# A product with V taken in five visits of a step instead of six, in an attention and mixture-of-experts layer

## The reference, cut to what matters

```python
x = _layernorm(resid_stream, ln_w, ln_b)                  # 4 x 1024 tokens, 128 wide
q = jnp.einsum('bsd,hde->bshe', x, W_q) + b_q             # 16 heads of 64
k = jnp.einsum('bsd,hde->bshe', x, W_k) + b_k
v = jnp.einsum('bsd,hde->bshe', x, W_v) + b_v
scores = jnp.einsum('bqhe,bkhe->bhqk', q, k) * scale
scores = jnp.where(causal, scores, -jnp.inf)              # a query sees keys up to its own
pattern = jax.nn.softmax(scores, axis=-1)
z = jnp.einsum('bhqk,bkhe->bqhe', pattern, v)
attn_out = jnp.einsum('bqhe,hed->bqd', z, W_o) + b_o
```

## Time and profile before

| What | Value |
|---|---|
| median of 3 runs | 1194.63 us (1191.52 to 1194.76) |
| the profiled execution's own time | 1196.98 us |
| its span, first to last instruction | 1195.3 us |
| mean granted TensorE clock | 0.971 of 2.4 GHz |
| busy share of the span | PE 91%, DVE 77%, ACT 59%, POOL 53% |
| chain that ended last, by engine | PE 73%, DVE 10%, DMA 6% |

### The profile page before, as it was taken

One profiled execution on the slowest core, in us unless ns is written; L12 is line 12 of the kernel. 1 busy time (PEld: TensorE's weight loads), 2 busy tenths in 40 slices (PEclk: granted clock), 3 DMA queues, 4 the chain that ended last, 5 costly groups with the idle time before them and its releaser, 6 DMA issues.

```text
span 1195.3 us, 51556 instructions
## 1 busy us (share of the span) xinstructions
PE 1085.8 (91%) x19964; PEld 776.9 (65%) x19964; DVE 916.5 (77%) x2215; ACT 710.1 (59%) x1489; POOL 629.1 (53%) x634
## 2 busy tenths in 40 slices
PE   4799999999999999999999999999999557999995
PEld 2567777777777777677777777777776445445442
DVE  7878888888888888788888888888888573565653
ACT  4656666656666666566656665666666243576663
POOL 5866666565656665656555555555566121023232
PEclk8899999999999999999999999999999877999997
DMA  8667776666777767677777776677777530000000
GB/s 186 169 169 168 179 169 163 163 163 163 169 174 167 171 163 172 161 172 171 173 172 171 165 169 163 163 163 174 168 171 170 125 68 10 1 10 18 9 10 25
DMA packets 121358, 164.53 MB, mean 138 GB/s; under 512 B 44272, under 2 KB 55536, under 8 KB 121328
## 3 DMA queue, kind: packets, MB, share of 16 engines
q1 hardware_dynamic: 121328, 164.15, 58.1%
HBM read 109.28 MB, written 21.23 MB: 109 GB/s over the span
## 4 chain that ended last, share of the span: by engine, by line
PE 73%; DVE 10%; DMA 6%; issue 5%; ACT 3%; SPq 2%; POOL 1%; DVEq 0%; ACTq 0%; POOLq 0%
PE ZB L622 25%; PE SPS L605 13%; PE SPS L606 10%; DMA XTB<-xt_scratch 5%; DVE PTZ L914 5%; PE ZB L590 5%; PE ZB L595 5%; PE ZB L800 3%; PE ZB L630 2%; PE SPS L792 2%; DVE SSB L974 2%; SPq L415 1%; PE ZB L784 1%; PE ZB L818 1%; PE SPS L757 1%
## 5 line engine op out<-in xcount | busy, mean ns | idle before, releaser
L974 DVE CUSTOM_DVE_ANT_0 SSB<-SPS,MASK 128x640 f32<-128x640 f32 (+7 forms) x512 | 374.1, 747 | 149.5 <-PE SPS L606 126.5
L605 PE MATMUL SPS<-KHP,QS 128*128 (+2 forms) x768 | 330.0, 434 | 33.5 <-DVE NM L974 28.1
L1283 ACT ACTIVATE PRL<-SSB,NM 128x640 f32<-128x640 f32 (+3 forms) x256 | 252.7, 987 | 161.2 <-DVE NM L974 98.2
L622 PE MATMUL ZB<-PTZ,VR 32*64 32x256 f32 (+2 forms) x16384 | 329.5, 296 | 18.9 <-DVE PTZ L914 18.9
L622 PEld LDWEIGHTS ZB<-PTZ,VR 32*64 32x64 f32 x16384 | 265.2, 131 | 73.3 <-issue 58.7
L459 POOL TENSOR_TENSOR X<-X,OT 128x512 f32 (+1 forms) x64 | 82.0, 1281 | 355.2 <-ACT OT L1293 346.7
L606 PE MATMUL SPS<-KLP,QS 128*128 (+2 forms) x768 | 261.4, 349 | 0.0
L914 DVE STREAM_TRANSPOSE PTZ<-PRL 128x640 f32<-128x640 f32 (+3 forms) x256 | 255.1, 1025 | 0.0
L605 PEld LDWEIGHTS SPS<-KHP,QS 128*128 128x128 f32 x768 | 145.7, 190 | 123.2 <-issue 58.5
L1283 ACT ACTIVATE PRS<-SSB,NM 128x128 f32<-128x128 f32 (+3 forms) x256 | 142.2, 556 | 118.1 <-DVE NM L974 117.7
L442 POOL TENSOR_TENSOR QS<-RAW,QS 64x512 fp32r<-64x512 f32 x128 | 165.1, 1290 | 10.3
(11 more groups left out here) (171 smaller groups left out, 1085.6 us busy)
## 6 DMA issues: line engine op xcount, KB each, us to landing
VR<-v_scratch SPq DMA_DIRECT2D x256, 256.0 KB, 5.5
KHP<-KHP SPq DMA_DIRECT2D x64, 256.0 KB, 3.2
KLP<-KLP SPq DMA_DIRECT2D x64, 256.0 KB, 3.9
v_scratch<-V SPq DMA_DIRECT2D x32, 512.0 KB, 7.6
RSB<-rcp_scratch SPq DMA_DIRECT2D x64, 256.0 KB, 3.9
XTB<-xt_scratch SPq DMA_DIRECT2D x62, 256.0 KB, 3.2
WQK<-in_W_q SPq DMA_DIRECT2D x33, 64.0 KB
WQK<-in_W_k SPq DMA_DIRECT2D x33, 64.0 KB
```

The source lines that it names most:

```text
L605: pe.matmul(SP_[n % 2][:, c0:c0 + wc], q, kh[:, c0:c0 + wc], start=True, stop=False)
L622: last = pe.matmul(ZB[h * DH:(h + 1) * DH, i, kt * TR:QT * TR], VR[rows, j, kt, h * DH:(h + 1) * DH], turned_block(h, kt, j, rows), start= ...
L974: v.tensor_tensor_reduce(out=SSB[n % 2][:, 0:w], in0=SP_[n % 2][:, 0:w], in1=MASK[:, S - w:S], scale=1.0, scalar=BIG, op0=ALU.add, op1=ALU ...
L1283: act.activation(exps_of(n), SSB[n % 2][:, 0:w], ACT.Exp, bias=NM[:, col:col + 1], scale=-1.0, accum_out=L[:, col:col + 1]).then_inc(exp_d ...
```

## The change

It moves instructions in the two hand-written orders and removes or adds none. On PE, V0 and V1 are made in one visit. The pairs of score units that stood between visits stay pairs, but every pair now stands one visit earlier relative to V2 and later blocks (V2 follows S(5), S(6) where V1 did), and S(13) and S(14), which stood alone on the two sides of V6 and V7, now both follow V7.

On DVE the transpositions follow: turn(0) and turn(1) come before mask(5), the later pairs one place earlier relative to the masks, and turn(9) stands behind the four zn instructions.

```diff
@@ pe_step
-            values(0)
+            values(0, 1)
             scores(5, 6)
...
-            values(1)
+            values(2)
             scores(7, 8)
...
-            values(2)
+            values(3)
             scores(9, 10)
...
-            values(3)
+            values(4, 5)
             scores(11, 12)
-            values(4, 5)
-            scores(13)
             values(6, 7)
             if first:
                 pe_bias(pe)
-            scores(14)
+            scores(13, 14)
             v_of(0)
             v_of(1)
@@ dve_step
-            mask(5)
+            if first:
+                mask(5)
+            turn(0, 1)
+            if not first:
+                mask(5)
             mask(6)
             stats(2)
-            turn(0, 1)
+            turn(2, 3)
             stats(3)
             mask(7)
             mask(8)
-            turn(2, 3)
+            turn(4, 5)
             stats(4)
             mask(9)
             mask(10)
-            turn(4, 5)
+            turn(6, 7)
             stats(5)
             mask(11)
-            turn(6, 7)
+            turn(8)
             mask(12)
-            turn(8, 9)
             stats(6)
             if first:
                 dve_bias(v)
             for k in range(4):
                 zn(k)
+            turn(9)
             stats(7)
```

## The result

The changed kernel took 1181.94 us (median of 4 runs, 1179.43 to 1184.51), the kernel before 1193.82 in the same session. The ratio is 0.990, with a 95% interval of 0.9875 to 0.9919: faster by 1.0%, where 1183 was forecast. The profiled execution took 1184.51, and its span is 1182.8. A second comparison on another chip gave 0.987 (0.9837 to 0.9904).

A forecast was written before the change was run, and what follows sets the result against it. A PE-then-DVE loop was taken to set a 28.50 us floor, with late XTB transfers on top. Gains of 11.2 in the loop + 1.0 - 0.3 = 11.9 took 1194.63 to 1182.7, rounded 1183; range 1179 to 1187.

The forecast's parts named there:

- The joint: PE, V0 with V1 in one visit: saves 0.20 us per step, bounds 0 to 0.4.
- the prediction's own rival: PE, V0 and V1 together take what they took apart: floor stays, 1192, no change; chance 0.13.
- Scores: PE behind V7: S(13) takes 0.91 and S(14) 0.92, so v_of starts at 17.07 instead of 17.69.
- DVE: DVE's walk in a step: mask(5) at 4.2, mask(11) 13.21, zn 15.82, mask(13) 17.90 instead of 18.07.
- The floor: Shortest loop period, PE to V7's end, then DVE's tail: falls by 0.17, from 28.50 to 28.33.
- the rival on the clock: Longer PE idle before V0 brings 1.2 GHz: 1203.5, or 1236 in all 31 steps; chance 0.08 with another late handover.
- The fetch of XTB: SP's fetch behind v_of is issued 0.6 earlier; eleven long steps gain 0.6 each, 6.6.
- the first rival: XTB lands when it did, whatever the moment of issue: only the floor's gain, 5.1, and 0.7 at the ends; 1189; chance 0.15.
- The first step: S(13) now follows pe_bias, so v_of and the first fetch may be late: a loss of 0.3.
- The last step: DVE: turns 6 and 7 fall into the 12.45 wait before mask(11): a gain of 1.0, possibly nothing or 2.

The follow-up runs named there:

- pe_only: PE's order of the changed kernel with DVE's order of the kernel before; 1226.5 us, 1.024 of the kernel before.
- turn9_before_zn: The changed kernel with turn(9) back in front of zn, behind mask(12); 1192.3 us, 0.995 of the kernel before.
- t1: The changed kernel with turn(8) in front of mask(11) and turn(9) in front of zn, behind mask(12); 1174.6 us, 0.983 of the kernel before.
- early_turns: The changed kernel with turn(4) before mask(7), turns 5 and 6 behind mask(8), turns 7 to 9 behind mask(10); 1175.9 us, 0.982 of the kernel before.
- after_again: The changed kernel run once more without an edit, on another chip; 1181.7 us, 0.987 of the kernel before.
- first_old: The changed kernel with PE's first step alone as before: scores(13), pe_bias, scores(14); 1180.3 us, 0.987 of the kernel before.
- bias_late: The changed kernel with three of POOL's four additions to X moved to the start of the last step; 1183.3 us, 0.989 of the kernel before.
- v_first: The changed kernel with v_of in front of S(14); 1188.6 us, 0.994 of the kernel before.

## Why the prediction was right, and where it was not

**The joint.** V0 with V1 takes 3.43; the forecast had 1.9 + 1.7 - 0.2 = 3.4. S(11) at 12.08 is the walked number. The row of two blocks after the last step gave the right price. The stated range did not follow from the stated bounds: with a joint of nothing the prediction's own rival gives 1192, and by the same walk one of 0.4 gives about 1177, where the range was 1179 to 1187.

**Scores.** S(13) and S(14) were walked at 0.91 and 0.92; they take 0.91 and 0.93. `v_of` comes at 17.10 (17.07).

**DVE.** Right up to mask(13): mask(5)'s lateness is gone by mask(11), DVE is what is late at zn, mask(13) at 17.94 (17.90). pe_only shows the half of this in a run: with DVE's old order mask(13) is 1.15 later and the kernel 2.4% slower than before.

**The floor** was the term of wrong size: 0.17 forecast, 0.28 measured, 29 x 0.11 = 3.2 us. Of the 0.28, 0.13 are mask(13)'s (18.07 to 17.94) and 0.15 lie behind it (10.43 to 10.28). The failing step is "Behind mask(13) DVE's work is unchanged, V0 waits for the same turn(15)". In the kernel before DVE did not run without a pause there. Its rows in the same step are:

```profile
524.72 0.25 DVE L974 CUSTOM_DVE_ANT_0 SSB<-SPS,MASK 128x128 f32<-128x128 f32 x1
...
525.02 0.42 DVE L974 CUSTOM_DVE_ANT_0 SSB<-SPS,MASK 128x256 f32<-128x256 f32 x1
```

Mask(2) starts 0.30 behind mask(1); in the changed kernel it starts 0.19 behind it:

```profile
547.90 0.25 DVE L972 CUSTOM_DVE_ANT_0 SSB<-SPS,MASK 128x128 f32<-128x128 f32 x1
...
548.09 0.42 DVE L972 CUSTOM_DVE_ANT_0 SSB<-SPS,MASK 128x256 f32<-128x256 f32 x1
```

The last product of S(2) starts at 524.57 before and at 547.46 after, 0.45 and 0.63 ahead of mask(2). Where mask(2) waits for S(2) the distance is 0.45 to 0.46 (turn9_before_zn, t1, early_turns), so 0.45 marks a mask(2) that PE held up. So the old floor was PE's, by way of S(2), by 0.11, and the change made S(2) 0.45 earlier against V0.

The same sentence goes on that PE waits about 0.4 longer for turn(15), and the rival on the clock took its 1.0 of idle time before V0 from it. This did not come: V0's wait stayed at 0.62. Turn(15) stands right behind mask(2), for which S(4) waits too; PE's extra time went in front of S(3).

**The fetch of XTB.** The mechanism holds, shown by turn9_before_zn and v_first. Its gain, measured as what lies above the shortest periods, is 6.9 in the first pair of executions (11.2 to 4.3; the other three executions with the changed order in the loop, after_again, first_old and bias_late, have 4 to 7, and of the kernel before there is only one). The waits themselves fell only from 7.0 to 5.1, since PE reaches qk(1), which stands right ahead of qk(2), 0.70 earlier too (22.68 behind V0, 23.38 before): transfer and PE moved ahead together, and since PE now has room before mask(2), part of each wait costs nothing. The forecast booked it together with the floor; apart from 29 x 0.17 its terms held 5.7 for the 29 later periods. Had `XTB` kept its place (the first rival), turn9_before_zn would have cost only its 0.14 per step.

**The first step** was forecast as 0.3 late. Its first V0 came 1.44 early in one execution and 0.15 early in the other, and the first period (35.51 and 32.97) is no fixed property of the change. In the profiled pair it hid 4.6 us of gain; without it the loop's gain exceeds the forecast by about 4.

**The last step.** From mask(11) to mask(13) DVE takes 6.61 (7.54 before), the 0.9 to 1.0 forecast. Behind the last V0 only 0.64 of it is left, and that stretch differs by up to 6.5 us among the profiled kernels (259.8 to 266.3), so the end result of this term can't be told.

**The rivals.** The visit is not free, `XTB` did not keep its place, and V0 stays at full rate in the loop (3.43 for V0 and V1). The rival on the clock named something real, a wait behind which PE runs at the lower level, but it came behind single waits of 2.4 us and more in the first steps, and in the last step as before (V0 and V1 take 5.09 there), not behind 0.6 in every step.

The total was close partly by luck: the middle of the loop gained some 4 us more than forecast, and the first period of the profiled execution took 4.6 back.

## What to carry to other kernels

When two engines meet at one point of a loop, price a reordering on both at once: here either half alone made the kernel slower, by 2.4% and 0.6%, and the two together 1.0% faster. Ask of every instruction that is moved off the wait on one side what it frees on the queue behind it: in the first pair of traces nearly half of the loop's gain came from a transfer, and the PE work that needs it, coming 0.7 us earlier in the step, and turn(9) on the wrong side of zn lost it. Before calling a floor one engine's, look for pauses of a tenth of a microsecond in its "unbroken" tail, and don't read a single profiled start-up period as an effect of the change.

## What the runs showed of the hardware that was not expected

In the first pass through the loop's code PE stops for up to 3.0 us between two products of one group, a wait that the profile ascribes to nothing. In after_again, in which this stop is 2.17, the DMA view of 80 to 83.2 us has one packet on an instruction queue beside the data:

```profile
q8 instruction: 1, 0.02, 2.4%
```

From 130 to 900 us, in the later passes of the same loop, it has none, and PE does not stop so again. But such packets do not mark the stop: the changed kernel has them in the first pass as well, in the microseconds from 75 and from 82, and PE does not stop there. That the stop is a fetch of code is not shown, and its cause stays open.

After PE's wait of 4.65 for `XTB` in t1 its clock is at the lower of its two levels. Busy by stretch there (stretch, length, PE, PEld, DVE, ACT, POOL, clock, DMA share, GB/s):

```profile
88.00:91.00 3.00, 2.09 (x4) 1.06 (x5) 0.00 (x0) 0.00 (x0) 2.26 (x2) 0.50 1.10 205
```

The granted clock of 0.50 is 1.2 GHz. The length of the wait alone doesn't tell it. The first fetch of `XTB` in bias_late, PE idle by 2.41 before it, and in after_again, by 3.49:

```profile
55.35 2.07 PE L595 MATMUL ZB<-XTB,WQK 128*128 128x512 f32 x2 [2.41 <-DMA XTB<-xt_scratch]
```

```profile
55.55 1.12 PE L590 MATMUL ZB<-XTB,WQK 128*128 128x512 f32 x2 [3.49 <-DMA XTB<-xt_scratch]
```

The shorter wait was followed by the half rate, the longer was not. The Trainium skill, "TensorE: Matmul & The Clock Gate", section "The HAM clock gate", says that the engine falls to half rate when idle; the traces show the fall in t1 and bias_late and none in after_again, where the granted clock is 1.00 from 52 to 60 us, so a single idle time of this length did not settle it here, and the gaps of 0.6 in every step of the loop did not bring it about.
